# Two-layer experts behind cross-attention: the second layer turned over, and where its gate runs

## What is computed

```
x  = x + attention(ctx, layernorm(x)) @ Wout          # x: (2, 512, 128)
x2 = layernorm(x)
probs  = softmax(x2 @ Wg)                              # (2, 512, 8)
top_vals, top_idx = top_k(probs, 2); top_vals /= sum(top_vals)
mask, scores = scatter of 1 and of top_vals to (2, 512, 8)
h   = relu((x2 * mask[e]) @ W1[e] + b1[e])             # W1[e]: 128 x 256
y   = h @ W2[e] + b2[e]                                # W2[e]: 256 x 128
out = x + sum over e of y * scores[e]
```

## Time and profile before

| | |
|---|---|
| median of three runs | 345.75 us (345.21 to 346.17) |
| profiled execution | 345.02 us |
| its span, first to last instruction | 343.3 us |
| granted clock of TensorE | 1.000 of full |
| busy: PE, DVE, POOL, ACT | 336.5, 271.0, 253.9, 193.6 us |

### The profile page before, as it was taken

How to read it: one execution, slowest core, us unless ns; L and a number is a source line. 1 busy time by engine, 2 the same in 40 slices (tenths; PEclk the granted TensorE clock), 3 DMA queues, 4 the chain that set the end, 5 groups by cost and what they waited for, 6 DMA issues and landing times.

```text
span 343.3 us, 6128 instructions
## 1 busy us (share of the span) xinstructions
PE 336.5 (98%) x2351; PEld 231.3 (67%) x2351; DVE 271.0 (79%) x430; ACT 193.6 (56%) x257; POOL 253.9 (74%) x163
## 2 busy tenths in 40 slices
PE   7899999999999999999999999999999999999996
PEld 6675657574757566575747565665684478999896
DVE  5989757988999999999879797979728998267333
ACT  2464768484947567584849485665803544045341
POOL 5639999999999999999999899989884772110000
PEclk9999999999999999999999999999999999999999
DMA  4730000000010000000000000000000000000000
GB/s 127 212 97 2 0 0 4 0 17 0 2 31 17 15 2 0 3 1 2 0 17 2 1 0 17 0 2 0 2 3 0 1 32 1 2 0 2 31 3 31
DMA packets 6713, 5.81 MB, mean 17 GB/s; under 512 B 743, under 2 KB 5789, under 8 KB 6685
## 3 DMA queue, kind: packets, MB, share of 16 engines
q1 hardware_dynamic: 6389, 5.29, 5.0%
q10 hardware_dynamic: 296, 0.13, 0.1%
HBM read 4.89 MB, written 0.52 MB: 16 GB/s over the span
## 4 chain that ended last, share of the span: by engine, by line
PE 94%; DVE 2%; ACT 1%; DMA 1%; issue 0%; POOL 0%; DVEq 0%
PE xo L415 25%; PE sc L395 21%; PE mx L619 8%; PE sc L401 6%; PE sc L321 6%; PE sc L323 5%; PE sc L322 5%; PE mx L352 3%; PE xo L352 3%; PE mx L506 2%; PE xo L506 2%; PE xo L424 2%; PE mx L322 1%; PE mx L321 1%; PE mx L323 1%; PE xo L430 1%
## 5 line engine op out<-in xcount | busy, mean ns | idle before, releaser
L1144 POOL TENSOR_TENSOR psum_acc<-psum_acc,probs 111x1024 f32<-111x1024 f32 x63 | 161.4, 2561 | 9.3 <-DVE psum_acc L866 1.9
L688 ACT ACTIVATE probs<-sc 111x1024 f32<-111x1024 f32 x96 | 98.2, 1027 | 18.9 <-PE sc L401 11.4
L415 PE MATMUL xo<-probs,v_sb 111*64 111x512 f32 x384 | 88.2, 596 | 0.0
L395 PE MATMUL sc<-q_pair,k_pair 64*111 64x512 f32 x576 | 85.9, 401 | 0.8 <-ACT v_sb L678 0.4
L395 PEld LDWEIGHTS sc<-q_pair,k_pair 64*111 64x111 f32 x576 | 44.6, 171 | 29.1 <-issue 12.2
L415 PEld LDWEIGHTS xo<-probs,v_sb 111*64 111x64 f32 x384 | 26.2, 137 | 42.3 <-issue 38.7
L877 DVE RECIPROCAL recips<-recips 128x128 f32<-128x128 f32 x64 | 54.0, 904 | 0.0
L843 DVE TENSOR_REDUCE part_max<-mx 128x2 f32<-128x888 f32 x32 | 34.6, 1081 | 18.0 <-PE mx L352 16.6
L1144 POOL TENSOR_TENSOR psum_acc<-probs 111x1024 f32<-111x1024 f32 x16 | 38.4, 2398 | 8.0 <-ACT probs L688 8.0
L704 ACT COPY recips<-xo 128x512 f32<-128x512 f32 x16 | 9.4, 585 | 56.8 <-PE xo L424 48.8
L401 PE MATMUL sc<-max_row,ones_r 64*111 64x512 f32 x192 | 38.2, 390 | 0.0
(11 more groups left out here) (179 smaller groups left out, 521.2 us busy)
## 6 DMA issues: line engine op xcount, KB each, us to landing
w_raw<-in_L_ffn_W SPq DMA_DIRECT2D x8, 128.0 KB, 2.4
x_tok<-in_x SPq DMA_DIRECT2D x2, 256.0 KB, 3.1
wv_raw<-in_L_xattn_Wkv SPq DMA_DIRECT2D x4, 128.0 KB, 3.4
wout_sb<-in_L_xattn_Wout SPq DMA_DIRECT2D x1, 512.0 KB
wqk_raw<-in_L_xattn_Wq SPq DMA_DIRECT2D x7, 64.0 KB, 2.0
wqk_raw<-in_L_xattn_Wkv SPq DMA_DIRECT2D x7, 64.0 KB, 2.1
out<-x_tok SPq DMA_DIRECT2D x1, 256.0 KB, 2.0
out<-x_tok SPq DMA_DIRECT2D x2, 128.0 KB, 1.7
```

Source lines behind the costliest of these rows:

```text
L395: pe.matmul(sc[0:KP, kt % 2, h, :], k_pair[r, s % QKB, k_part, at], q_pair[r, s % QKB, q_part, :], start=(k_part + q_part == 0), stop=False)
L415: mm = pe.matmul(o_ps[h * HD:(h + 1) * HD, :], v_sb[0:KP, s // 2 % 2, kt, at:at + HD], probs[0:KP, e % RING, h, :], start=(kt == 0), stop= ...
L688: act.activation(probs[0:KP, e % RING, :, :], sc[0:KP, kt % 2, :, :], ACT.Exp).then_inc(exp_done, 1)
L1144: pool.tensor_tensor(psum_acc[0:KP, s % 2, :, :], first, probs[0:KP, e % RING, :, :], ALU.add) \
```

## The change

- Layer two is turned over. w2 is split into high and low parts and stands; the hidden values, split too, move as 512 tokens. An expert is six fp32r matmuls of 512 columns (`layer_two`). It is issued two experts behind layer one (`LAG` = 2).
- The hidden values are split by: ReLU of half 0 into SBUF, its high part on ACT, its low part on POOL (`low_first`); ReLU of half 1 in place in PSUM, high part on ACT, low part on DVE (`low_second`).
- Features now lie on partitions in y, so a score is needed for each token along the row. `turn_scores` and `copy_scores` give rows of scores; SP writes them to DRAM (`score_rows`) and reads back one broadcast of 128 partitions for each expert, into `spread` (over the memory of `probs`; batch 1's over batch 0's as they come free).
- `add_expert` is a product y x spread into `scaled` and a sum into `acc_t` (two DVE instructions of 512, each waiting for the one before). At the end of a batch PE turns `acc_t` back (`turn_acc`) and DVE adds it to x1 (`add_rows`); the last expert goes in two halves. The bias is one matmul, b2 standing.
- The gate's operands lie in PSUM, one of each instruction at least; one more product is made so. `split_x2` makes high part, low part and copy all on DVE.
- Order. `turn_x2(0)` stands ahead of step 15's dots and `logits(0)` behind them; x1 and its norms come ahead of reciprocals on DVE; POOL does gather 3. Batch 0's scores turn at g = 0, bias at g = 1. The output projection of batch 1 moves to g = 2 (seven pairs) and 3 (the last). `turn_x2(1)` is at g = 5, `logits(1)` at 6, the gate's exponential on ACT behind expert 6, `gate_end(1)` on DVE at g = 7, `turn_scores(1)` on PE at g = 9, ahead of layer two of expert 7, and the bias at 10.
- W1's high parts go from POOL to ACT, one for each of eight steps, and its low parts stay on POOL. w2's high parts are made by ACT at steps 11 to 14, its low parts by POOL at step 14 and amid the first experts.

```diff
-W1_AT = {2: 0, 3: 1, 9: 2, 11: 3}
+W1_AT = {2: 0, 3: 1, 8: 2, 9: 3, 10: 4, 11: 5, 12: 6, 13: 7}
+W2_HI_AT = {11: (0,), 12: (1, 2), 13: (3, 4), 14: (5, 6, 7)}
+LAG = 2
...
+        x2_ps = [mx[:, 0, :], pj]
+        rank_ps = [mx[:, 0, :], pj]
+        score_ps = [mx[:, 1, :], o_ps]
...
         def _(sp):
...
+            for b in range(B):
+                sp.wait_ge(score_copied, b + 1)
+                if b == 0:
+                    sp.wait_ge(added, (KT - 1) * STEPS)
+                sp.dma_start(score_rows[b], score_t[:, b, :]).then_inc(rows_out, 16)
+                sp.wait_ge(rows_out, 16 * (b + 1))
+                for e in range(E):
+                    if b:
+                        sp.wait_ge(y_scaled, e + 1)
+                    sp.dma_start(spread[:, e, :], score_rows[b, e].partition_broadcast(P)).then_inc(spread_in[e], 16)
...
         def _(pe):
...
-            def hidden(g):
+            def layer_one(g):
...
+                    elif c == 0:
+                        pe.wait_ge(r0_done, g - 1)
                     else:
+                        pe.wait_ge(lo1_done, g - 1)
...
+            def layer_two(g):
+                e = g % E
+                if g >= 2:
+                    pe.wait_ge(y_scaled, g - 1)
...
+                pe.wait_ge(w2_split, min(g + 1, E))
+                for half, at in enumerate(halves if g == B * E - 1 else [slice(0, N)]):
+                    y = y_ps(g, half)[:, at]
+                    for c, hi_done, lo_done in ((0, hi0_done, lo0_done), (1, hi1_done, lo1_done)):
+                        n = (g * HC + c) % FR
+                        pe.wait_ge(hi_done, g + 1)
+                        pe.matmul(y, w2_hi(e)[:, c, :], relu_hi[:, n, at], start=(c == 0), stop=False)
+                        pe.matmul(y, w2_lo(e)[:, c, :], relu_hi[:, n, at], start=False, stop=False)
+                        pe.wait_ge(lo_done, g + 1)
+                        mm = pe.matmul(y, w2_hi(e)[:, c, :], relu_lo[:, n, at], start=False, stop=(c == HC - 1))
+                    mm.then_inc(y_ready, 1)
...
             for g in range(B * E):
-                hidden(g)
+                layer_one(g)
+                if g == 0:
+                    turn_scores(0)
                 if g == 1:
+                    bias_term(0)
                     pe.wait_ge(o_copied, STEPS)
                     total(s, o_ps)
-                if g >= 1:
-                    expert_out(g - 1)
+                if g == 9:
+                    turn_scores(1)
+                if g >= LAG:
+                    layer_two(g - LAG)
                 if g == 2:
                     pe.wait_ge(sum_copied, STEPS)
+                    pe.wait_ge(o_norm, STEPS - 1)
+                    out_project(1, x1_ps[1], range(PAIRS - 1))
+                if g == 3:
+                    pe.wait_ge(o_norm, STEPS)
+                    out_project(1, x1_ps[1], range(PAIRS - 1, PAIRS))
+                if g == 5:
+                    turn_x2(1)
                 if g == 6:
-                    turn_x2(1)
-                if g == 7:
                     logits(1)
+                if g == 10:
+                    bias_term(1)
+                if g == 12:
+                    turn_acc(0, 0, range(QT))
...
         def _(act):
...
             for g in range(B * E):
-                for c in range(HC):
-                    relu(g * HC + c)
+                relu_first(g)
+                high_first(g)
+                relu_second(g)
+                high_second(g)
+                if g in (0, 9):
+                    copy_scores(g // E)
                 if g == 1:
                     copy_sum(STEPS - 1, o_ps)
                 if g == 6:
-                    copy_x2(1)
-                if g == 7:
                     gate_exp_of(1)
...
         def _(dve):
...
             def split_x2(b):
-                dve.wait_ge(x2_hi, b + 1)
-                dve.tensor_tensor(kv_lo[:, b, 0:N], pj[:, :], kv_hi[:, b, 0:N].bitcast(F32),
+                dve.wait_ge(x2_turned, b + 1)
+                chained(dve.tensor_copy(kv_hi[:, b, 0:N], x2_ps[b]))
+                dve.tensor_tensor(kv_lo[:, b, 0:N], x2_ps[b], kv_hi[:, b, 0:N].bitcast(F32),
                                   ALU.subtract).then_inc(x2_lo, 1)
+                dve.tensor_copy(kv_t[:, b, 0:N], x2_ps[b]).then_inc(x2_copied, 1)
...
+                dve.tensor_tensor(scaled[:, g % 2, at], y_ps(g, half)[:, at], spread[:, e, at], ALU.mult) \
+                   .then_inc(y_scaled, 1)
+                dve.wait_ge(y_scaled, g + half + 1)
...
+                dve.tensor_tensor(acc_t(b)[:, at], scaled[:, g % 2, at], acc_t(b)[:, at] if e else pj,
+                                  ALU.add).then_inc(acc_v, 1)
...
             for g in range(B * E):
-                add_expert(g)
...
+                low_second(g)
+                if g == 4:
+                    norm_x1(1)
+                if g >= LAG:
+                    add_expert(g - LAG)
+                if g == 1:
+                    for c in range(RC):
                         reciprocal(STEPS - 1, c)
                 if g == 3:
                     x1_and_moments(1, x1_ps[1])
-                if g == 4:
-                    norm_x1(1)
                 if g == 5:
                     split_x2(1)
                 if g == 6:
                     gate_start(1)
+                if g == 7:
                     gate_end(1)
+                if g == 12:
+                    add_rows(0, 0, slice(0, QT), 1)
...
         def _(pool):
...
+            for g in range(B * E):
+                if g == 4:
+                    rstd_x1(1)
+                    pool.wait_ge(normed_ready, NORMED0 + QT * B)
+                low_first(g)
+                if g == 0:
+                    normalise(STEPS - 2)
+                if g == 2:
+                    normalise(STEPS - 1)
+                if g < E - 2:
+                    w2_low(g + 2)
```

326 lines of the change are left out of this document (184 added, 142 removed).

## The result

The changed kernel takes 351.92 us in the median (349.43 to 352.4) against 345.52 of the kernel before on the same chip: ratio 1.0167, interval 1.0125 to 1.021, so 1.7% slower. The direction was as forecast, the size was not: 347.8 was predicted, and the median lies 0.4 us above the range's upper end of 351.5. (The forecast was held against a kernel before of 345.75; the ratio of 1.0167 laid on that gives 351.5, just that end.) The profiled execution is the shortest of them, 349.43 us with a span of 347.6; the others have spans of 349.5 to 350.7 at a mean granted clock of 0.987 to 0.989 instead of 0.994. That gap inside one kernel needed an explanation of its own, and got most of one only in the last experiment. One execution of the version with the earlier gate, further down, took 470.16 us at a granted clock of 0.656 and is left out of its numbers.

A forecast was written before the change was run, and what follows sets the result against it. TensorE, busy 98% of the span, was taken as the bound. Stage 56.4 us free of pauses plus waits made 64.9 against 64.2; with 0.5 port, 0.2 start and 1.4 tail, span 346.1, plus 1.7 gives 347.8 us; range 341.8 to 351.5.

The forecast's parts named there:

- two bias terms: Expert stage on PE: 8 small matmuls each time, 2.3 us in all, become one wide matmul, about 1.0; 1.3 less.
- small waits: Expert stage: its pieces add up to 0.8 us less than its 64.2; these waits between them taken as gone.
- layer one and two of an expert: Steady expert on PE: 2 x 1.40 = 2.80 us instead of 3.18, 6.1 us less over 16 experts.
- wait, logits of batch 1: PE reaches batch 1's logits at 304.2 us, DVE has x2 in SBUF at 306.4: 2.2 us waited.
- the port: DVE's additions with two SBUF operands slowed beside POOL, experts 3 to 9: 0.5 us, bounds 0 and 2.5.
- wait, score turn: PE asks for batch 1's scores at 314.2 us, DVE's gate ends at 318.1: 3.9 us waited.
- wait, last layer two: Last layer two on PE waits for expert 13's multiplication, behind low part 15 on DVE: 0.85 us.
- last matmul to the end: Tail of half product, half sum, two transposes, half sum and store: 4.2 us instead of 2.84, 1.4 more.
- The rival with the falling clock: PE's clock falls in the 3.9 us score-turn pause: 2.8 to 5.6 us more, 352 us; chance 0.04.
- rival (a): DVE keeps up, batch 1's two gate waits shrink to 1 us or so: 342.3 us; chance 0.24.
- rival (b): Each addition blocked by POOL's low part, broadcasts later than DVE's request; ten experts cost 4 us: 351.5 us; chance 0.15.
- Rival (c): Layer two's six matmuls miss 1.40 us and take 1.70, as now: about 349 us; chance 0.05.

The follow-up runs named there:

- the last experiment: Repeat trace of the changed kernel with batch 0's score copy moved ahead of expert 0's second ReLU: 351.44 us; also called the second look.
- the version with the earlier gate: Changed kernel with batch 1's output projection whole ahead of layer two of expert 0, its gate an expert or so earlier, gate's end in two pieces: 348.55 us, ratio 1.0096.
- w2's parts early: Changed kernel, but POOL makes w2's low parts of experts 4 to 7 in one go during batch 1's output projection: 351.57 us, ratio 1.0187.
- the second look: Same kernel as the early score copy, run again unedited for another trace: 351.44 us, clock 0.989.
- the early score copy: Changed kernel, but ACT copies batch 0's turned scores ahead of the second ReLU of expert 0: 349.67 us, ratio 1.0139.
- the product in PSUM: Changed kernel, but the score-output product stays in its PSUM bank for 10 of 16 experts, so the addition reads one SBUF operand: 349.75 us, ratio 1.012.
- the last two versions: Everything early with batch 1's score turn behind layer two of expert 7: 343.53 us; then also its turn of x2 one step later: 342.33 us.
- the run again: The changed kernel unedited, for a second trace and more times: 350.56 us, ratio 1.0165.
- the kernel kept busy: Changed kernel with matmuls nobody reads in PE's two pauses, ahead of batch 1's logits and score turn: 352.14 us, ratio 1.0199.
- everything early: Changed kernel with early gate, w2's parts early, product in PSUM, batch 0's score copy and expert 13's addition moved ahead: 344.28 us, ratio 0.998.
- no gate for batch 1: Changed kernel without batch 1's logits, ranking, exponential, score turn and broadcasts; batch 0's scores are used for batch 1: 342.71 us, ratio 0.9933.

## Why the prediction was right in direction and short in size

The bound, the gain and the place of the loss were right. PE was the bound; layer two is 2.80 us an expert, 6.1 less in all; and the gain went into waits of PE for DVE, first at the logits and then at the score turn, as the forecast had it. DVE near 95% was seen from 300 to 308 us (98%) and from 316 to 320 (93%), but not between (1.58 of 4 us from 308 to 312).

The mechanism held, and several terms of the sum were mis-sized. Of the 4.1 us between 347.8 and 351.92, 1.6 lie in the profiled execution: the two bias terms and the "small waits", counted as 2.1 us of gain, gave 0.06, and the matmuls at the lower clock and the longer end, put at nothing and at 4.2, took 1.55 and 5.0; the shorter wait at the score turn hid most of that. The other 2.5 lie between the profiled execution and the median. The sum put this step at nothing, although it had noted 0.7 us for it in the kernel before.

By the steps of the sum, predicted against the profiled execution (us):

| step | predicted | measured |
|---|---|---|
| experts start | 276.4 | 275.95 |
| layer one and two of an expert | 2.80 | 2.80 |
| two bias terms | 1.3 less | 0.06 less |
| "small waits" that go | 0.8 less | 0 |
| wait, bias of batch 0 | 0.7 | 0.60 |
| wait, turn of x2 | 0.85 | 0.59 |
| wait, logits of batch 1 | 2.2, and 0.5 for the port | 2.81 |
| wait, score turn | 3.9 | 1.40 |
| wait, last layer two | 0.85 | 0.53 |
| matmuls at the lower clock | 0 | 1.55 |
| last matmul to the end | 4.2 | 5.0 |

*The bias term.* I set the 2.3 us of the earlier trace rows against 1.0 for the new ones together. A new one costs 1.05 us by itself (323.27 to the next matmul at 324.32), and an old one cost 1.08, for 2.16 in all. It is an fp32 product, and its width does not make it cheap: two records of 0.5 us for 512 columns where a split matmul needs 0.23. The step had mistaken the shape for the price.

*The small waits.* The 0.8 us did not go. Where a narrow form is followed by a wide one, the first wide matmul takes 0.32 instead of 0.23 us (277.80 to 278.12). The steady expert of before has one such place inside its 3.18; the new one has none, but nine others are left between the experts, at the turns, bias terms and pieces of the projection: an estimated 0.8 us.

*The port.* The mechanism was named and its rows were the right ones, but at 0.5 us it was sized too low: 1.06 in the chain to the logits, 2.7 in the version with the early gate. In the changed kernel 2 of the 16 additions were lengthened, those at 301.79 and 304.30 us. For the early gate the bound of 2.5 was nearer than my 0.5.

*The score turn.* The scores came at 318.3 us, forecast 318.1. PE did not come at 314.2 but at 317.2: 1.05 later from the logits and 1.6 from the lower clock. So the wait was 1.4 instead of 3.9, and the fall of the clock was paid out of it.

*The end.* The sum left out that DVE still has the product and the addition of expert 14 (341.51 to 342.92) ahead of the first half of expert 15, while PE's last matmul ends at 342.61. So the product of the last half starts at 343.63, 1.0 us behind that end. That is the 0.8, and the 0.3 by which the forecast's own terms (3.9) fall short of its 4.2.

These differences are 1.2 + 0.8 - 0.45 - 2.6 (waits; the port is in them) - 0.5 + 1.55 + 0.8 = 0.8, which takes 346.1 to 346.9; 0.7 of the measured span of 347.6 is left. An estimate for it is what the five pauses lay bare: a wide matmul's record runs 0.39 us where the next one starts after 0.23, and ahead of a pause the other 0.16 counts too, 0.8 in all.

*The clock.* The rival with the falling clock had 4%, and was sized at 2.8 to 5.6 us. It happened in each of the seven traces with this order of the gate, behind the first wait and not the second; in the usual execution it costs nothing, at double length 1.5 us. The argument against it, that PE's clock had never fallen, was no evidence, since the kernel before makes no pause in this stage and the change was forecast to make one of 3.9. The Trainium skill's rule on inactivity in "TensorE: Matmul & The Clock Gate", section "What's actually happening", was quoted beside it and should have had a larger chance. The step from the profiled 349.43 to the median of 351.92, 2.5 us, is most likely this: 1.5 for more of the lower clock, and the attention loop's own 1.0. None of the longer executions of the changed kernel was traced. In other versions an execution at 0.988 or 0.989 had either one fall of double length (w2's parts early, and the second look at the early score copy) or two short ones (the product in PSUM); the second look and the product in PSUM put 1.5 us on either. A sum made for the profiled execution cannot contain it.

*The rivals.* That DVE keeps up was wrong for this order of work and is nearly what the last two versions reach: 343.53 and 342.33. That the latter is the 342.3 of rival (a) is a coincidence, since these versions hold other changes too. That the broadcasts delay was refuted for batch 1 (350.59 against 350.56). That additions are blocked by the low part was right as a mechanism; it lengthens DVE's chain by 1.06 us in the changed kernel and by 2.7 with the early gate. The 351.5 of rival (b) does not follow from its own terms (347.8 and 4 make 351.8), and that the measured median lies close to it is luck: the broadcasts that it counts on cost nothing for batch 1, and the blocked additions about 1 us. Rival (c), that layer two does not reach 1.40, did not come about: the expert took 2.80.

Not settled: whether the double fall follows from where the pause lies or from chance; half of the executions of the run again and of the early score copy were at 0.989 with nothing in the program different. Of the seven traces with this order of the gate, the first expert starts at 275.95 to 276.20 us in the four with one short fall, at 276.45 and 277.13 in the two with the double one, and at 276.96 in the one with two short falls. The later start and the longer time at the lower clock came together; that the one brings the other is not shown. That the short fall costs nothing rests on one full-clock execution and one trace of the kernel kept busy, which pays for its added matmuls as well, and on the version with the product in PSUM, whose executions at 1.000 (348.67 and 348.69) lie just the 1 us under the short ones of again that its shorter wait explains.

## What to carry to other kernels

A pause of the engine that bounds can be paid twice, because its clock may fall behind it. The pause's length alone did not decide that here: the clock fell in or behind waits of 2.5 to 3.3 us in every trace, behind 1.8 us with the product in PSUM and not with everything early, and not behind the 2.2 us of the kernel kept busy. So when work moves to helpers, write down for each wait what its operand's chain is, and put the consumer one independent block later rather than wait: here two such moves gave some 1.9 us and left the clock at 0.998 to 1.000. Count for every new VectorE operation how many of its operands lie in SBUF while GpSimd reads there; moving one to PSUM brought TensorE no new wait here. And when an operand form changes, price the new instruction from a row of its type, not of its shape.

## What was not expected of the hardware

- Behind a pause of 2.8 us TensorE's granted clock went to 1.2 GHz, in the changed kernel 1.9 us after work had begun again, and eight matmuls stood 0.43 us apart (in the second look the logits right behind the pause were slow already); behind the pause of 0.6 us ahead of the fp32 matmuls of the bias term it did so in two traces (no gate for batch 1, the product in PSUM) and not in others.
- The same program shows a fall of one length in some executions and of twice that length in others, 1.7 and 3.4 us of clock lost, with identical waits (the two traces of the early score copy); the longer one adds 1.5 us.
- A collision over SBUF holds both sides: on DVE 0.69 us became 1.16 to 1.81, ending 0.54 to 0.55 us behind the end of the POOL instruction that they met (1.16 with the early gate met a w2 part, the others low parts), and the w2 part that POOL began just then took 1.2 instead of 0.74. POOL's low parts kept their 1.3 us where they had begun first. Where the addition had (338.10, ahead of POOL's at 338.44 in the changed kernel), it kept its 0.69 and POOL's low part took 1.51.
